# Edge stage of a graph attention layer: visits of eight chunks instead of four, rings of four groups of eight

## The chip, the cores and the metric

One core of a Trainium2 chip runs the kernel. The metric is device time in microseconds for one execution. Engines are named PE (TensorE), DVE (VectorE), ACT (ScalarE), POOL (GpSimd) and SP (SyncE).

## The reference

6250 nodes with 256 features, 206250 edges sorted by destination node (100000 random edges, the same edges reversed, and one loop for each node). All data is float32.

```python
z = einsum('ni,hid->nhd', layernorm(x), W)          # 4 heads of 64
es, ed = (z * a_src).sum(-1), (z * a_dst).sum(-1)
e = leaky_relu(es[src] + ed[dst], 0.01)
alpha = softmax of e over the edges with one dst
x = x + segment_sum(alpha[:, :, None] * z[src], dst)
# then: layernorm, gate to 16 experts, top 2, w1 (256x512), relu, w2, + b2,
# weighted sum, residual, layernorm; x = x + that
```

## The kernel before

The program is a row of stages. Stage A normalises the nodes and multiplies them with W; each node leaves a row of 260 floats in `z_table` in HBM: 256 of z and 4 of es. The edge stage, which the change touches, takes about three quarters of the span. Then come the gate (stage C) and the experts.

In the edge stage a chunk is 128 edges, one to a partition. A group is G = 4 chunks. There are 403 groups (1612 chunks). The nodes are in 49 tiles of 128. A visit is a pair of a group and a node tile for which the group has edges: as the edges are sorted, that is one visit for each group and one more for each end of a tile, VISITS = FULL + NT = 402 + 49 = 451. The tables `visit_tile`, `visit_group`, `visit_word` and `visit_base`, made in stage A, say which group and tile visit v has. `group_free` says how many visits must be over before the buffers of a group may be used again.

The work of the engines in the edge stage:

- POOL, `gather`: for each group it waits on `b_msg` for the messages of an earlier group (four groups back, LEAD = 4), and then issues G indirect DMAs, one for each chunk, each of 128 rows of `z_table` into `ring[:, s, c, :]`. The ring has RING = 8 slots of G chunks.
- SP: for each group `relay` waits until its gathers have landed and counts `b_group` up. For each second group it also loads the destinations of two groups, one row sent to all partitions (`load_pair`, into `dst_bc`), as soon as `make_ST` is done with the groups that lie there, and `relay_pair` waits for that load and counts `b_rows` up. These steps stand in one written order: relay of an even group comes after the relay_pair in front of it.
- DVE, for visit v: `make_ST` (0/1 matrix of node by edge, 128 x G*128), `e_add`, `e_lrelu`, `e_shift`, `e_clamp` (the logits, 128 x 4G), `one_hot` (0/1 matrix of edge by node), `message` (z times weight, 128 x G*256), `accumulate` (adds the sum in PSUM to `acc`).
- PE, for visit v: `destination`, G matmuls that bring ed[dst] to the edges, and `weigh`, G matmuls of 260 columns that add the messages by node into one PSUM tile.
- ACT: `open_group` (copies es out of the ring; it waits for `b_group`), `locate`, `exponent`; near the end also `weight`, which divides finished tiles by their denominators, while DVE's `settle` adds them to x.

The whole stage is written out visit by visit by `written_out`. Each engine goes through iterations i, and in iteration i it runs each of its steps for visit i minus the lag of that step, in the order of the list. On DVE the lag of `make_ST` is 0, of the four logit steps AHEAD = 6, of `one_hot` and `message` AHEAD + 1, and of `accumulate` AHEAD + 1 + MSG_TO_ACC = AHEAD + 3. So `message` of visit v stands on DVE behind `e_add` of visit v + 1. SR = 8 is the number of buffers for S, ST and msg. `destination` of an even visit waits until the logits of visits up to v - SR + 1 are done, since two visits share a PSUM tile (`dest_of`). All of it runs once for each pass; the inputs need one pass.

Of the kernel before, what the change touches and what calls it, by code (L numbers as in the profile page):

```python
# [28 lines left out]
I32 = mybir.dt.int32  # L29
BF16 = mybir.dt.bfloat16  # L30
ALU = mybir.AluOpType
# [1 line left out]
AX = mybir.AxisListType  # L33

P = 128
G = 4
RING = 8
LEAD = 4
SLOPE = 0.01
EPS = 1e-5  # L40
LEVEL = 64.0
# [4 lines left out]
MSG_TO_ACC = 2  # L46
# [1 line left out]
TINY = 1e-30  # L48
RMAX = bass.bass_isa.ReduceOp.max
PAD_DST = 1 << 20  # L50
AHEAD = 6
ZR = 12
SOON = AHEAD + 1

# [49 lines left out]
def gnn_moe_kernel(nc, E, x, x_turned, src_cols, dst_cols, dst_flat, dst_last, W, a_src, a_dst, gate_w, gate_b, w1, b1, w2, b2, gamma, beta, out):  # L104
# [44 lines left out]
    with whole:  # L149
# [23 lines left out]
        visit_tile = sb(graph, "visit_tile", [1, VISITS], I32)  # L173
        visit_group = sb(graph, "visit_group", [1, VISITS], I32)
        visit_word = sb(graph, "visit_word", [1, VISITS], I32)
        group_free = sb(graph, "group_free", [1, GROUPS + RING - LEAD], I32)
        level = sb(graph, "level", [P, HEADS])
        npass_i = sb(graph, "npass_i", [P, 1], I32)

# [43 lines left out]
        with ExitStack() as ctx:  # L223
# [149 lines left out]
            def _(dve):  # L373
# [71 lines left out]
                def aside(t, s, r):  # L445
# [18 lines left out]
                    if t == TABLES + 6:  # L464
                        dve.wait_ge(a_cnt, 2)
                        step(nc.vector.tensor_scalar(visit_base[:, :], psA[1][:, 0:VISITS], -float(P), None, ALU.mult))
                        step(nc.vector.tensor_copy(visit_tile[:, :], psA[1][0:1, 0:VISITS]))
                        step(nc.vector.scalar_tensor_tensor(out=visit_group[:, :], in0=psA[1][0:1, 0:VISITS], scalar=-1.0,
                                                            in1=iota_f[0:1, 0:VISITS], op0=ALU.mult, op1=ALU.add))
                        step(nc.vector.tensor_scalar(visit_slot[:, :], visit_group[:, :], RING - 1, None, ALU.bitwise_and))  # L470
                        step(nc.vector.tensor_copy(visit_word[:, :], visit_slot[:, :]))
                        step(nc.vector.scalar_tensor_tensor(out=visit_word[:, MSG_TO_ACC:VISITS], in0=visit_tile[:, 0:VISITS - MSG_TO_ACC],
                                                            scalar=float(RING), in1=visit_slot[:, MSG_TO_ACC:VISITS], op0=ALU.mult, op1=ALU.add))
                        step(nc.vector.scalar_tensor_tensor(out=visit_word[:, 0:VISITS - SOON], in0=visit_group[:, SOON:VISITS],
                                                            scalar=float(RING * TILE_SPAN), in1=visit_word[:, 0:VISITS - SOON], op0=ALU.mult, op1=ALU.add))
                        step(nc.vector.memset(group_free[:, 0:RING], 0))
                        step(nc.vector.tensor_tensor(group_free[:, RING - 1:GROUPS + RING - LEAD], psA[2][0:1, 0:GROUPS - LEAD + 1],
                                                     iota_f[0:1, 0:GROUPS - LEAD + 1], ALU.add))
                    if t == EARLY + 5:
                        dve.wait_ge(a_edges[0], 16)  # L480
                        step(nc.vector.tensor_scalar(dst_mod[:, :], dst_raw[:, :], P - 1, None, ALU.bitwise_and))
# [60 lines left out]
        b_stats = sem("b_stats"); b_var = sem("b_var")  # L542
        SETTLED = 3 * PART
        CLOSED = VISITS - 1 - (NT - SETTLED)
        assert CLOSED >= 0 and CLOSED + 11 >= 2 * 8 + (VISITS - 2 * 8) // 8 * 8
        SH = 2 * HEADS
        PASS_STEPS = 8
        FIN_STEPS = 2 + BULK - 1
        SR = 8
        with ExitStack() as ctx:  # L550
            nodes = sb(ctx, "nodes", [P, NT, SH])
            decided = sb(ctx, "decided", [P, NT, HEADS])
# [3 lines left out]
            stats_b = decided[:, :, :].rearrange("p t h -> p (t h)")[:, 0:PART * 6].rearrange("p (t c) -> p t c", c=6)  # L556
            ring = sb(ctx, "ring", [P, RING, G, ROW])
            es_edge = sb(ctx, "es_edge", [P, 4, G, HEADS])
            S = xs[:, KEPT:KEPT + 2 * SR, :].rearrange("p (s o) c -> p s (o c)", o=2).rearrange("p s (g e) -> p s g e", g=G)
            ST = xs[:, KEPT + 2 * SR:KEPT + 4 * SR, :].rearrange("p (s o) c -> p s (o c)", o=2)  # L560
            dst_bc = sb(ctx, "dst_bc", [P, RING, G * P], BF16)
            earg = sb(ctx, "earg", [P, 4, 3, G * HEADS])
            msg = sb(ctx, "msg", [P, SR, G, ROW])
# [62 lines left out]
            def _(pool):  # L626
                npass = pool.value_load(npass_i[0:1, 0:1], min_val=1, max_val=PASSES_MAX)
                with pool.Fori(0, npass) as k:
                    def gather(g, s, r):

                        done = pool.value_load(group_free[0:1, bass.ds(g + RING - LEAD, 1)], min_val=0, max_val=VISITS)
                        pool.wait_ge(b_msg, done + 1)
                        pool.sem_inc(apart, 1)
                        for c in range(G):
                            at = src_idx[:, g * G + c:g * G + c + 1]
                            nc.gpsimd.indirect_dma_start(ring[:, s, c, :], None, z_table,  # L636
                                                         bass.IndirectOffsetOnAxis(ap=at, axis=0)).then_inc(b_landed[s], 16)
                    for g in range(GROUPS):
                        gather(g, g % RING, g // RING)
                    pool.sem_inc(b_over, 1)  # L640
                    pool.wait_ge(b_go, k + 1)

            @block.vector
            def _(dve):
# [5 lines left out]
                with dve.Fori(0, npass) as k:  # L650
# [115 lines left out]
                    def accumulate(v, s, r):  # L766
# [5 lines left out]
                        if not early(v, 1):  # L772
                            dve.wait_ge(b_acc, v)
                        at = acc[:, bass.ds(tile, 1), :].rearrange("p o c -> p (o c)")
                        nc.vector.tensor_tensor(at, at, psM[s % 2][:, 0:ROW], ALU.add).then_inc(b_acc, 1)  # L775
                    written_out(VISITS, SR, [(settle, 11), (look_up, AHEAD + 1), (e_add, AHEAD), (make_ST, 0), (e_lrelu, AHEAD),
                                                       (accumulate, AHEAD + 1 + MSG_TO_ACC), (e_shift, AHEAD), (one_hot, AHEAD + 1),
                                                       (e_clamp, AHEAD), (message, AHEAD + 1)])
                    dve.wait_ge(b_acc, VISITS)
# [6 lines left out]
            def _(act):  # L786
                npass = act.value_load(npass_i[0:1, 0:1], min_val=1, max_val=PASSES_MAX)
                with act.Fori(0, npass) as k:
# [29 lines left out]
                    def weight(v, s, r):  # L818
# [5 lines left out]
                        for t in range(n * BATCH, (n + 1) * BATCH):  # L824
# [1 line left out]
                                at = acc[:, t, h * DH:(h + 1) * DH]  # L826
                                last = nc.scalar.activation(at, at, ACT.Copy, scale=rden_b[:, t, h:h + 1])
                            last.then_inc(b_scaled, 1)
                    written_out(VISITS, SR, [(open_group, AHEAD + 2), (locate, AHEAD + 3), (exponent, AHEAD + 3), (weight, 12)])
                    act.sem_inc(b_over, 1)  # L830
                    act.wait_ge(b_go, k + 1)

# [702 lines left out]
```

## Time and profile before

| what | us |
|---|---|
| median of three runs | 2792.49 (2790.86 to 2793.21) |
| the profiled execution, its own time | 2791.16 |
| its span in the profile | 2789.3 |
| busy in the span: PE / DVE / POOL / ACT | 2258.7 / 1711.3 / 1849.1 / 682.4 |
| granted TensorE clock, mean (1 is 2.4 GHz) | 0.821 |
| first gather of the edge stage / last gather | 80.65 / 2126.79 |
| first instruction of stage C | 2147.7 |

Times in the rows are in microseconds from the start of the span, unless they are durations; a mean or a minimum in a row is in ns. A group of instructions has its busy time, the mean of one, and behind the last bar the idle time of the engine just before them with what ended it ("issue" is nothing that the profile shows). A busy engine is not for that reason the bound: the bound is found by following who waits for whom.

### The profile page before, as it was taken

The numbers are of one execution on the slowest core, as the hardware profiler recorded it, in microseconds if no ns is written. First come the engines' busy times: TensorE is split into PE (matmuls) and PEld (weight loads), VectorE is DVE, ScalarE is ACT, GpSimd is POOL, SyncE is SP. The second block draws the span as 40 slices with busy tenths as digits, with TensorE's granted clock in tenths as the row PEclk, the third lists the DMA queues.
The fourth block names the chain that finished last, engine by engine and source line by source line (L and its number), as shares of the span: only waits on it lengthen the run. The fifth ranks groups of instructions, "written<-read, shape, count | busy, mean of one in ns | idle before, by whom it ended". The sixth has DMA issues, their size and how long they took to land. (4 is left out here: it accounts for less than half of the span.)

```text
span 2789.3 us, 54969 instructions
## 1 busy us (share of the span) xinstructions
PE 2258.7 (81%) x10829; PEld 1890.7 (68%) x10830; DVE 1711.3 (61%) x4828; ACT 682.4 (24%) x2857; POOL 1849.1 (66%) x1949
## 2 busy tenths in 40 slices
PE   7688787877878788887888888777884848999997
PEld 5576666666666666666766666666663818999985
DVE  6666666666666666666666666666666674333336
ACT  4111111111111111111111111111115415555557
POOL 0677777777777777777777777777774025555547
PEclk9677888788787887888787788888877559999998
DMA  9444444445454444555454554444554207633328
GB/s 315 121 133 133 130 133 131 133 133 132 132 133 133 133 132 130 133 133 133 133 134 134 133 133 133 132 128 133 134 132 127 87 0 243 197 103 106 107 93 278
DMA packets 183503, 382.70 MB, mean 137 GB/s; under 512 B 38837, under 2 KB 86880, under 8 KB 182474
## 3 DMA queue, kind: packets, MB, share of 16 engines
q0 software_dynamic: 87744, 243.02, 32.6%
q1 hardware_dynamic: 79656, 122.51, 13.7%
q10 hardware_dynamic: 15842, 14.43, 2.0%
q8 instruction: 74, 1.21, 0.2%
q14 instruction: 187, 1.53, 0.2%
HBM read 345.87 MB, written 33.93 MB: 136 GB/s over the span
## 5 line engine op out<-in xcount | busy, mean ns | idle before, releaser
L636 POOL DMA_INDIRECT ring<-z_table,src_idx x1612 | 1556.4, 965 | 496.0 <-issue 458.1
L858 PE MATMUL psMb<-msg,xs 128*128 128x260 f32 x3608 | 1202.5, 491 | 255.4 <-DVE msg L761 253.5
L858 PEld LDWEIGHTS psMb<-msg,xs 128*128 128x128 f32 x3608 | 827.1, 241 | 432.4 <-DVE msg L761 284.0
L847 PEld LDWEIGHTS psEb<-nodes,xs 128*128 128x128 f32 x3608 | 550.0, 224 | 269.3 <-issue 238.2
L847 PE MATMUL psEb<-nodes,xs 128*128 x3608 | 522.7, 272 | 156.5 <-DVE xs L688 155.9
L761 DVE TENSOR_TENSOR msg<-ring,psPb 128x1024 f32<-128x1024 f32 x451 | 546.4, 1211 | 0.0
L807 ACT COPY es_edge<-ring 128x16 f32 x451 | 91.8, 204 | 1679.2 <-SPq L583 1642.6
L702 DVE TENSOR_TENSOR earg<-es_edge,psEb 128x16 f32<-128x16 f32 x451 | 76.1, 169 | 559.5 <-ACT es_edge L807 555.4
L694 DVE TENSOR_TENSOR xs<-iota_f,psPb 128x512 f32<-128x512 f32 x451 | 305.9, 678 | 0.1
L688 DVE TENSOR_SCALAR xs<-dst_bc,iota_p 128x512 f32 x451 | 229.9, 510 | 99.5 <-issue 95.2
L1275 POOL DMA_INDIRECT rows_sb<-norm_rows,src_sb x108 | 109.8, 1017 | 168.1 <-DVE src_sb L1352 149.7
L1307 PE MATMUL psHd<-xT,w_sb 128*128 128x128 f32 x1728 | 213.2, 277 | 0.0
L775 DVE TENSOR_TENSOR acc<-acc,psMb 128x260 f32 x451 | 188.1, 417 | 36.8 <-PE psMb L858 31.4
L1319 PE MATMUL psYd<-w_all,hid 128*128 x864 | 204.4, 380 | 0.3 <-ACT hid L1342 0.3
L1307 PEld LDWEIGHTS psHd<-xT,w_sb 128*128 128x128 f32 x1728 | 204.2, 194 | 0.1
L1363 DVE COPY xT<-psXd 128x256 f32<-128x256 f32 x108 | 45.9, 425 | 255.9 <-PE psXd L1297 255.9
L1319 PEld LDWEIGHTS psYd<-w_all,hid 128*128 128x128 f32 x864 | 156.1, 191 | 17.3 <-issue 0.5
L1330 ACT COPY w_sb<-w_all 128x1024 f32 x108 | 112.8, 1045 | 156.7 <-PE psHd L1307 96.6
L1282 POOL DMA_INDIRECT pair_rows<-y_sb,dst_sb x108 | 107.0, 991 | 45.5 <-issue 36.1
L1342 ACT ACTIVATE hid<-psHd,b1T 128x128 f32<-128x128 f32 x432 | 123.6, 368 | 34.1 <-issue 25.9
L796 ACT ACTIVATE psPb<-dst_col,visit_base 128x4 f32 x451 | 120.5, 267 | 1.4 <-issue 1.4
L814 ACT ACTIVATE msg<-earg 128x16 f32<-128x16 f32 x451 | 91.0, 202 | 54.2 <-DVE earg L720 49.5
(209 smaller groups left out, 1413.3 us busy)
## 6 DMA issues: line engine op xcount, KB each, us to landing
dst_bc<-dst_rows SPq DMA_DIRECT2D x202, 256.0 KB, 3.5
ring<-z_table,src_idx POOLq DMA_INDIRECT x1612
w_all<-in_L_ffn_w_dram SPq DMA_DIRECT2D x32, 512.0 KB
b_sb<-in_L_ffn_b_dram ACTq DMA_DIRECT2D x108, 128.0 KB, 3.1
got<-pair_rows SPq DMA_DIRECT2D x48, 256.0 KB, 4.2
xs<-in_x_dram SPq DMA_DIRECT2D x5, 1536.0 KB, 10.9
z_table<-z_out SPq DMA_DIRECT2D x49, 130.0 KB, 6.3
norm_rows<-xnc SPq DMA_DIRECT2D x49, 128.0 KB, 1.7
```

Of the source, the lines that this page charges most:

```text
L636: nc.gpsimd.indirect_dma_start(ring[:, s, c, :], None, z_table, bass.IndirectOffsetOnAxis(ap=at, axis=0)).then_inc(b_landed[s], 16)
L688: nc.vector.tensor_scalar(ST[:, s, :], dst_bc[:, bass.ds(slot, 1), :].rearrange("p o f -> p (o f)"), iota_p[:, 0:1], None, ALU.is_equal).t ...
L694: nc.vector.tensor_tensor(S[:, s, :, :], over(iota_f[:, 0:P].unsqueeze(1), [P, G, P]), over(psP[s % 2][:, G * HEADS:G * HEADS + G].unsquee ...
L761: nc.vector.tensor_tensor(msg[:, s, :, 0:D].rearrange("p g (h d) -> p g h d", h=HEADS), ring[:, bass.ds(slot, 1), :, 0:D].rearrange("p o g ...
L775: nc.vector.tensor_tensor(at, at, psM[s % 2][:, 0:ROW], ALU.add).then_inc(b_acc, 1)
L796: nc.scalar.activation(psP[s % 2][:, G * HEADS:G * HEADS + G], dst_col[:, bass.ds(group * G, G)], ACT.Identity, bias=visit_base[:, v:v + 1])
L847: last = nc.tensor.matmul(dest_of(s)[:, c * SH:(c + 1) * SH], ST[:, s, c * P:(c + 1) * P], nodes[:, bass.ds(tile, 1), :].rearrange("p o c ...
L858: last = nc.tensor.matmul(psM[s % 2][:, 0:ROW], S[:, s, c, :], msg[:, s, c, :], start=c == 0, stop=c == G - 1)
L1307: last = nc.tensor.matmul(psH[s % 2][:, f * P:(f + 1) * P], w1_sb[:, s % 2, c, f * P:(f + 1) * P], xT[:, s % 2, c, :], start=c == 0, stop= ...
L1319: last = nc.tensor.matmul(psY[s % 2][:, 0:D], hid[:, s % 2, f, :], w2_f, start=f == 0, stop=f == FC - 1)
L1330: nc.scalar.copy(w1_sb[:, s % 2, :, :].rearrange("p c f -> p (c f)"), w_all[:, bass.ds(e, 1), 0:KD * F].rearrange("p o f -> p (o f)")).the ...
L1342: last = nc.scalar.activation(hid[:, s % 2, f, :], psH[s % 2][:, f * P:(f + 1) * P], ACT.Relu, bias=b1T[:, bass.ds(e, 1), f:f + 1].rearran ...
```

## The change

G goes from 4 to 8 and RING from 8 groups to 4, so that the ring holds the same 32 chunks. SR goes from 8 to 4 and AHEAD from 6 to 3, in visits of twice the size. LEAD goes away: a gather waits for the messages of the group four back, which now is the one in the same slot. There are 202 groups (1616 chunks) and VISITS = 201 + 49 = 250. `accumulate` stays two visits behind `message` (MSG_TO_ACC = 2), which are now two visits of eight chunks. PAIRED = RING // 2 goes from 4 to 2 pairs of `dst_bc`, each load twice as large (512 KB over all partitions in place of 256 KB). The lags of `settle` and `weight` are written in terms of AHEAD.

```diff
--- before.py
+++ after.py
@@ -33,9 +33,8 @@
 AX = mybir.AxisListType
 
 P = 128
-G = 4
-RING = 8
-LEAD = 4
+G = 8
+RING = 4
 SLOPE = 0.01
 EPS = 1e-5
 LEVEL = 64.0
@@ -48,7 +47,7 @@
 TINY = 1e-30
 RMAX = bass.bass_isa.ReduceOp.max
 PAD_DST = 1 << 20
-AHEAD = 6
+AHEAD = 3
 ZR = 12
 SOON = AHEAD + 1
 
@@ -173,7 +172,7 @@
         visit_tile = sb(graph, "visit_tile", [1, VISITS], I32)
         visit_group = sb(graph, "visit_group", [1, VISITS], I32)
         visit_word = sb(graph, "visit_word", [1, VISITS], I32)
-        group_free = sb(graph, "group_free", [1, GROUPS + RING - LEAD], I32)
+        group_free = sb(graph, "group_free", [1, GROUPS + 1], I32)
         level = sb(graph, "level", [P, HEADS])
         npass_i = sb(graph, "npass_i", [P, 1], I32)
 
@@ -474,8 +473,8 @@
                         step(nc.vector.scalar_tensor_tensor(out=visit_word[:, 0:VISITS - SOON], in0=visit_group[:, SOON:VISITS],
                                                             scalar=float(RING * TILE_SPAN), in1=visit_word[:, 0:VISITS - SOON], op0=ALU.mult, op1=ALU.add))
                         step(nc.vector.memset(group_free[:, 0:RING], 0))
-                        step(nc.vector.tensor_tensor(group_free[:, RING - 1:GROUPS + RING - LEAD], psA[2][0:1, 0:GROUPS - LEAD + 1],
-                                                     iota_f[0:1, 0:GROUPS - LEAD + 1], ALU.add))
+                        step(nc.vector.tensor_tensor(group_free[:, RING - 1:GROUPS + 1], psA[2][0:1, 0:GROUPS - RING + 2],
+                                                     iota_f[0:1, 0:GROUPS - RING + 2], ALU.add))
                     if t == EARLY + 5:
                         dve.wait_ge(a_edges[0], 16)
                         step(nc.vector.tensor_scalar(dst_mod[:, :], dst_raw[:, :], P - 1, None, ALU.bitwise_and))
@@ -542,11 +541,12 @@
         b_stats = sem("b_stats"); b_var = sem("b_var")
         SETTLED = 3 * PART
         CLOSED = VISITS - 1 - (NT - SETTLED)
-        assert CLOSED >= 0 and CLOSED + 11 >= 2 * 8 + (VISITS - 2 * 8) // 8 * 8
+        assert CLOSED >= 0
         SH = 2 * HEADS
         PASS_STEPS = 8
         FIN_STEPS = 2 + BULK - 1
-        SR = 8
+        SR = 4
+        SPAN = G * P // D
         with ExitStack() as ctx:
             nodes = sb(ctx, "nodes", [P, NT, SH])
             decided = sb(ctx, "decided", [P, NT, HEADS])
@@ -556,8 +556,8 @@
             stats_b = decided[:, :, :].rearrange("p t h -> p (t h)")[:, 0:PART * 6].rearrange("p (t c) -> p t c", c=6)
             ring = sb(ctx, "ring", [P, RING, G, ROW])
             es_edge = sb(ctx, "es_edge", [P, 4, G, HEADS])
-            S = xs[:, KEPT:KEPT + 2 * SR, :].rearrange("p (s o) c -> p s (o c)", o=2).rearrange("p s (g e) -> p s g e", g=G)
-            ST = xs[:, KEPT + 2 * SR:KEPT + 4 * SR, :].rearrange("p (s o) c -> p s (o c)", o=2)
+            S = xs[:, KEPT:KEPT + SPAN * SR, :].rearrange("p (s o) c -> p s (o c)", o=SPAN).rearrange("p s (g e) -> p s g e", g=G)
+            ST = xs[:, KEPT + SPAN * SR:KEPT + 2 * SPAN * SR, :].rearrange("p (s o) c -> p s (o c)", o=SPAN)
             dst_bc = sb(ctx, "dst_bc", [P, RING, G * P], BF16)
             earg = sb(ctx, "earg", [P, 4, 3, G * HEADS])
             msg = sb(ctx, "msg", [P, SR, G, ROW])
@@ -628,7 +628,7 @@
                 with pool.Fori(0, npass) as k:
                     def gather(g, s, r):
 
-                        done = pool.value_load(group_free[0:1, bass.ds(g + RING - LEAD, 1)], min_val=0, max_val=VISITS)
+                        done = pool.value_load(group_free[0:1, bass.ds(g, 1)], min_val=0, max_val=VISITS)
                         pool.wait_ge(b_msg, done + 1)
                         pool.sem_inc(apart, 1)
                         for c in range(G):
@@ -773,7 +773,7 @@
                             dve.wait_ge(b_acc, v)
                         at = acc[:, bass.ds(tile, 1), :].rearrange("p o c -> p (o c)")
                         nc.vector.tensor_tensor(at, at, psM[s % 2][:, 0:ROW], ALU.add).then_inc(b_acc, 1)
-                    written_out(VISITS, SR, [(settle, 11), (look_up, AHEAD + 1), (e_add, AHEAD), (make_ST, 0), (e_lrelu, AHEAD),
+                    written_out(VISITS, SR, [(settle, AHEAD + 2 + MSG_TO_ACC), (look_up, AHEAD + 1), (e_add, AHEAD), (make_ST, 0), (e_lrelu, AHEAD),
                                                        (accumulate, AHEAD + 1 + MSG_TO_ACC), (e_shift, AHEAD), (one_hot, AHEAD + 1),
                                                        (e_clamp, AHEAD), (message, AHEAD + 1)])
                     dve.wait_ge(b_acc, VISITS)
@@ -826,7 +826,7 @@
                                 at = acc[:, t, h * DH:(h + 1) * DH]
                                 last = nc.scalar.activation(at, at, ACT.Copy, scale=rden_b[:, t, h:h + 1])
                             last.then_inc(b_scaled, 1)
-                    written_out(VISITS, SR, [(open_group, AHEAD + 2), (locate, AHEAD + 3), (exponent, AHEAD + 3), (weight, 12)])
+                    written_out(VISITS, SR, [(open_group, AHEAD + 2), (locate, AHEAD + 3), (exponent, AHEAD + 3), (weight, AHEAD + 4)])
                     act.sem_inc(b_over, 1)
                     act.wait_ge(b_go, k + 1)
 
```

## Rows read from the trace of the kernel before

**Rows 1.** Busy time and count by stretch, granted clock, DMA share, GB/s.

```profile
80.00:97.00 17.00, 0.00 (x0) 0.00 (x0) 15.59 (x14) 1.49 (x2) 14.83 (x6) 0.50 0.30 94
97.00:2128.00 2031.00, 1645.89 (x7193) 1358.52 (x7193) 1341.11 (x3615) 298.60 (x1892) 1541.52 (x1607) 0.81 0.50 132
```

**Rows 2.** The gathers, line 636, from 97 to 2128 us: group, durations, idle before.

```profile
L636 POOL DMA_INDIRECT ring<-z_table,src_idx x1607 | 1541.8, 959 | 489.5 <-issue 456.9 <-DVE msg L761 32.6
...
L636 POOL DMA_INDIRECT ring<-z_table,src_idx x1607: 942/946/1583, 96.7 to 2126.8; - x179
...
  DVE msg L761: 32.6, 107
```

**Rows 3.** Who waited for whom, 97 to 2128 us: total, times, longest.

```profile
SPq L583 <- DMA ring<-z_table,src_idx: 1178.6, 401, 7.9
SPq L597 <- DMA dst_bc<-dst_rows: 635.2, 198, 3.9
...
DVE earg L702 <- ACT es_edge L807: 552.8, 333, 3.4
```

**Rows 4.** DVE's groups of instructions, 97 to 2128 us.

```profile
L761 DVE TENSOR_TENSOR msg<-ring,psPb 128x1024 f32<-128x1024 f32 x449 | 543.9, 1211 | 0.0
L694 DVE TENSOR_TENSOR xs<-iota_f,psPb 128x512 f32<-128x512 f32 x449 | 304.6, 678 | 0.1
L688 DVE TENSOR_SCALAR xs<-dst_bc,iota_p 128x512 f32 x451 | 229.9, 510 | 99.5 <-issue 95.2 <-PE psEb L847 3.7
L775 DVE TENSOR_TENSOR acc<-acc,psMb 128x260 f32 x447 | 186.4, 417 | 34.0 <-PE psMb L858 29.5 <-issue 3.5
L720 DVE TENSOR_SCALAR earg<-earg 128x16 f32<-128x16 f32 x450 | 86.2, 192 | 0.0
L702 DVE TENSOR_TENSOR earg<-es_edge,psEb 128x16 f32<-128x16 f32 x450 | 76.0, 169 | 556.9 <-ACT es_edge L807 552.8 <-PE psEb L847 2.9 <-issue 0.8
```

**Rows 5.** PE's groups, 97 to 2128 us.

```profile
L858 PE MATMUL psMb<-msg,xs 128*128 128x260 f32 x3585 | 1194.9, 491 | 252.2 <-DVE msg L761 250.3
L847 PE MATMUL psEb<-nodes,xs 128*128 x3608 | 522.7, 272 | 156.5 <-DVE xs L688 155.9
```

**Rows 6.** Timeline (start, duration): two pairs of make_ST and gather.

```profile
203.56 0.49 DVE L688 TENSOR_SCALAR xs<-dst_bc,iota_p 128x512 f32 x1 [0.27 <-issue]
203.66 1.21 POOL L636 DMA_INDIRECT ring<-z_table,src_idx  x1 [0.31 <-issue]
...
1003.51 0.49 DVE L688 TENSOR_SCALAR xs<-dst_bc,iota_p 128x512 f32 x1 [0.27 <-issue]
1003.52 0.94 POOL L636 DMA_INDIRECT ring<-z_table,src_idx  x1 [0.30 <-issue]
```

**Rows 7.** Loads by SP: one in time, landing of dst_bc, of other loads.

```profile
304.70 0.20 ACT L807 COPY es_edge<-ring 128x16 f32 x1 [2.12 <-SPq L583]
305.13 0.32 SPq L586 DMA_DIRECT2D dst_bc<-dst_rows  x1
...
DMA to landing us min/median/max: 3.1/3.5/4.3
...
acc<-in_x_turned_dram SPq DMA_DIRECT2D x12, 512.0 KB, 9.2
xs<-in_x_dram SPq DMA_DIRECT2D x3, 512.0 KB, 6.6
```

**Rows 8.** Timeline of the stage's end.

```profile
2126.79 0.95 POOL L636 DMA_INDIRECT ring<-z_table,src_idx  x1 [0.30 <-issue]
2130.46 0.17 DVE L702 TENSOR_TENSOR earg<-es_edge,psEb 128x16 f32<-128x16 f32 x1 [2.60 <-ACT es_edge L807]
2134.03 8.70 ACT L827 ACTIVATE acc<-acc,pass_tmp 128x64 f32<-128x64 f32 x36
2137.46 2.02 PE L858 MATMUL psMb<-msg,xs 128*128 128x260 f32 x8 [0.58 <-DVE msg L761]
2139.62 0.42 DVE L775 TENSOR_TENSOR acc<-acc,psMb 128x260 f32 x1 [1.89 <-PE psMb L858]
```

## The prediction

> **What bounds the kernel now.** I read the busy times by stretch first. The edge stage's body runs from 97 to 2128 us, 2031 us of a span of 2789, and in it no engine is busy throughout: PE 1646, POOL 1542, DVE 1341 [rows 1]. Busy shares alone would point at PE. So next come the waits. DVE waits 553 us at `e_add` for ACT's copy of es [rows 3], ACT waits for SP's relay, and SP waits 1179 us for gathers to land [rows 3]. The chain leads to POOL. Its own group shows 1607 gathers of 959 ns in the mean, with 489.5 us of idle time, that is 0.305 us before each [rows 2]. Is this idle time a wait? 107 of the gaps are put down to `message`, but they too are 32.6/107 = 0.30 us long [rows 2], no longer than the others, which end on nothing that the profile shows. So POOL issues gathers back to back, one each 1.264 us (2031/1607), at group boundaries as elsewhere. 0.946 (the median) + 0.305 = 1.251 would be the period without disturbance; the mean of 959 is 13 ns over the median, in all 21 us over 1607 gathers. The edge stage lasts as long as POOL takes to issue its gathers, plus the way of the last one through the other engines. What the change does to DVE, PE, ACT and SP is worth nothing unless it reaches one of these: the number of gathers, their period, the end.
>
> **What disturbs a gather.** At 203.56 `make_ST` (line 688) begins, 0.10 us before a gather, and ends 0.39 us after the gather's start; that gather takes 1.21 us. At 1003.51 `make_ST` begins 0.01 us before a gather, and that one takes 0.94 [rows 6]. So a `make_ST` that is already under way holds the start of the gather up: 1.21 - 0.946 = 0.26 us for an end 0.39 us behind the start, hence delay = (end behind the start) - 0.13. With D the length of `make_ST` and starts spread evenly over a period of 1.25 us, one of them costs (D - 0.13)^2 / 2.5. For D = 0.49 [rows 6] (the mean of 0.510 in [rows 4] has `make_ST`'s own delays in it) that is 0.052 us, times 451 = 23 us, against the 21 found above. The two agree, so I take this as the source of the excess.
>
> The Trainium skill, page "SBUF — State Buffer", section "SBUF: two separate sides", has such a rule: a DVE instruction in a 2-port mode, or with two SBUF inputs, takes the port pair shared with GpSimd for the whole instruction, and GpSimd cannot write descriptors meanwhile. The slow gather agrees with it; the 0.94 us gather beside a `make_ST` started just before does not fit a lock over both whole instructions. Held strictly, the rule would charge each `make_ST` its full length: 250 of them by the 0.80 us worked out below, near 200 us.
>
> **The change, part by part.** The sum is made against the profiled execution, 2791.16 us (span 2789.3); the median of the runs is 1.3 us above it.
>
> 1. Gathers. 202 groups of 8 are 1616, 403 groups of 4 were 1612. The four more are padding but are issued. POOL: 4 x 1.25 = +5.0 us, all on the path.
>
> 2. Group overhead on POOL (value_load, wait, counter) is halved, but it costs nothing now: the gap is 0.30 us inside groups and between them. 0 us. It could give at most nothing, as there is no longer gap to remove.
>
> 3. `make_ST`. A 16-wide instruction of this kind costs 0.192 (line 720), the 512-wide one 0.49 [rows 4, 6], so 0.30/496 = 0.60 ns an element, and 1024 cost 0.80 us. Half as many, each longer. Evenly spread: 0.67^2/2.5 = 0.18 us x 250 = 45 us, against 21 to 23: +22 to +24. But the starts are not spread evenly: `make_ST` follows `e_add`, and that follows the landing of a group's last gather, so most are at nearly one phase of POOL's period. [rows 6] show how narrow it is: 0.10 us before the gather costs 0.26 us, 0.01 before costs nothing. In the new kernel a hit at that phase costs 0.80 - 0.10 - 0.13 = 0.57 us, a miss nothing. For some 75 visits (second visits of a group and those behind an SP load) I take the even 0.18: 13 us. For the other 175, the even cost of 0.052 in the old kernel over a hit's 0.26 makes one in five a hit: 35 x 0.57 = 20 us. Together 33 us, against 21: +12 us. Bounds: no hit at all, -21 us; a hit each time for the 175, 100 + 13 - 21 = +92 us. I take +12, nearest to what the rows show on average.
>
> By the Trainium skill, page "VectorE: DVE Perf Modes", section "Mode 2×_2P — use both read ports for one tensor", such a one-input float32 result comes two elements a cycle at 0.96 GHz, so 512 more would be an estimated 0.27 us, not 0.31. The trace's slope is close to this. By the page the sum would be some 4 us less.
>
> 4. DVE. `message` over 2048: 1.211 + 1024 x (1.211 - 0.417)/764 = 2.28 us; `one_hot` 0.678 + 0.53 = 1.21; `make_ST` 0.80; `accumulate` 0.417 as before; four small ones some 0.19 each [rows 4]. That is 5.4 us a visit, 250 visits 1350 us, against 3.5 x 451 = 1579. DVE is relieved of some 229 us, off the path: it had 553 us of waiting for gathers, and it gets more. For a group of 8 (8 x 1.264 = 10.1 us of POOL) it has 1.24 visits, 6.7 us. 0 us.
>
> 5. PE. 2000 chunk visits by 0.491 + 0.272 [rows 5] are 1526 us, before 1804, 1376. +150 us, covered by the idle time of the body (2031 - 1646 = 385 us). Without that cover up to +150. `destination` of an even visit now waits for `e_clamp` of the third visit before it, in the same DVE iteration; before, that was an iteration back. It is late by about 2.5 us, and what is queued behind it on PE is `weigh`, whose message isn't ready sooner. 0 us.
>
> 6. SP. With AHEAD = 3, `make_ST` at the landing T of odd group g builds the visit three further on. If no group near is split, that is group g+3, in the pair that SP loads only after T. The issue is 0.43 us behind the es copy (304.70 to 305.13); 256 KB land in 3.5 us, other loads of 512 KB in 6.6 and 9.2 [rows 7]. Bounds 3.5 and 9.2, I take 5, since this one is the old load doubled; with the relay `make_ST` starts near T + 6.5. Behind it on DVE are `one_hot` and `message`, so the iteration ends at T + 11; the next group lands at T + 10.1 and its iteration is over at T + 16.5, before T + 20.2, the landing after it. Three whole groups without a tile's end are 1 - 3/4.1, about a quarter of the pairs. Does POOL feel it? A gather of group g+4 needs the last message of g, which stands behind `e_add` of g+1. The last gather before a landing starts 3.7 us ahead of it (2126.79 to 2130.46 [rows 8]), so gather g+4 starts 20.2 - 3.7 + 1.25 = 17.8 us after T(g+1). Message g ends 5.4 us after T(g+1), or 11 to 12 behind a late load. POOL doesn't wait: 0 us. Cover gone if the load takes over some 11 us.
>
> 7. The end. From the last `e_add` (2130.46) to ACT's last `weight` (2134.03 + 8.70) it was 12.3 us; DVE ended at 2139.62 + 0.42 [rows 8]. New: two iterations of DVE behind the landing, the last message some 8.5 us after it, then 8 matmuls of 0.505 (2.02/4) and `accumulate`: 13.1 us. ACT has fewer `weight` blocks left and is no longer last. +1 us (up to +6 if PE is at its lower clock there). The stage's head (six gathers up to 97 us [rows 1]) stays.
>
> Sum: 5.0 + 12 + 1 = +18 us. Against the profiled execution that is 2809; the median could lie 1 us higher, which I leave in the range.
>
> **The rivals.** What this kernel can tell from no change is 0.2%, 5.6 us.
> - *Fewer `make_ST`, fewer hits: faster.* 250 in place of 451, and their phase falls just behind a gather's start. For it: the phase is narrow and a longer es copy and `e_add` move it later, towards the harmless side. Against: DVE time under `make_ST` stays near 200 us. At no hits: 2791 + 6 - 21 = 2776. It decides if the disturbance falls below 9 us of the old 21. Chance 0.12.
> - *No change.* Hits as before: 2797, or a few less. Chance 0.18, for a sum within 5.6 us of the old.
> - *Phase locked on the bad side.* 2791 + 92 + 6: 2889; half of it 2843. For it: nearly all landings now have one phase. Chance 0.10 for over 2835.
> - *Late destination rows.* Landing of 512 KB over 11 us: POOL waits in a quarter of the 101 pairs, 2 us each for 13 us, +50: 2859. Against: 9.2 is the slowest row of that size. Chance 0.04.
> - *PE becomes the bound.* The body's granted clock is 0.81, between the levels of 1.2 and 2.4 GHz [rows 1]. 1.24 visits of 8 chunks cost 7.6 us of the 10.1 at that mean. At the lower level throughout, 0.81/0.5 of it, 12.3 us: +2.2 x 202 = 440 us. Against: PE would then have no idle time, and in the body it has 385 us. Chance 0.03.
>
> **How the numbers follow.** The likeliest case, slower by a longer hold on POOL and four more gathers, has 0.53; it gives 2809. With the three worse ones slower has 0.70, no change 0.18, faster 0.12. The likeliest case's own range is 2798 to 2830. For 8 in 10 I leave out the bad lock, the late rows and PE above (0.13 or so beyond 2838), and half of the faster case below: 2788 to 2838.
>
> **What would show it.** 1616 gathers, gap before each still 0.30; median duration 0.946 still, with fewer but longer slow ones (up to 1.5 us) and a mean near 966; `make_ST` near 0.80 us; DVE's busy time down by 200 us and its wait for es up; the body at 1616 periods. I am wrong if POOL shows gaps over 0.31 put down to `message`, if SP's wait for `dst_bc` has single values over 10 us, or if the mean gather comes below 950 ns.

## The result: 28 us slower, where 18 were forecast

The changed kernel takes 2819.88 us in the median (2818.54 to 2821.84, four runs), the kernel before beside it 2791.99. The ratio is 1.010 with an interval of 1.0087 to 1.0113. So the change makes the kernel 1.0% slower, by more than its runs scatter. The forecast was 2809, with 2788 to 2838 around it, and 0.70 for slower.

The page of the changed kernel, its span and engines:

```profile
span 2817.4 us, 46496 instructions
## 1 busy us (share of the span) xinstructions
PE 2313.0 (82%) x11613; PEld 1988.1 (71%) x11614; DVE 1589.9 (56%) x3220; ACT 566.7 (20%) x2053; POOL 1871.5 (66%) x1953
```

The busy times by stretch, to be read against [rows 1]:

```profile
78.00:95.00 17.00, 0.00 (x0) 0.00 (x0) 15.59 (x14) 0.00 (x0) 14.80 (x6) 0.50 0.30 94
95.00:2150.00 2055.00, 1699.38 (x7960) 1453.10 (x7961) 1219.79 (x2013) 190.78 (x1114) 1564.43 (x1611) 0.81 0.46 131
```

The body has grown by about 24 us, with PE busier (1699 us), DVE less so (1220), and POOL as before the engine without a wait of its own. Its gathers from 97 us on, beside the first row of [rows 2]:

```profile
L636 POOL DMA_INDIRECT ring<-z_table,src_idx x1610 | 1563.6, 971 | 490.4 <-issue 445.9 <-DVE msg L761 44.5
```

Mean 971 ns instead of 959; 490.4 us of gaps over 1610 gathers are 0.305 us each, as before, and none of the 1616 gathers has more than 0.31 us before it. So the gaps have not changed; the gathers themselves have become longer. The waits of the other engines in the same stretch, in the form of [rows 3], first by engine, then by SP's queue:

```profile
DVE earg L702 <- ACT es_edge L807: 652.9, 198, 6.6
...
DVE xs L688 <- SPq L597: 121.3, 28, 5.1
...
POOL ring L636 <- DVE msg L761: 44.5, 146, 0.3
```

```profile
SPq L583 <- DMA ring<-z_table,src_idx: 1577.9, 201, 18.4
SPq L597 <- DMA dst_bc<-dst_rows: 370.6, 99, 4.6
```

DVE waits 100 us longer for landings than it did. 28 times `make_ST` waits for SP's load of destination rows, 4.3 us each. The load itself, with the new `make_ST` (durations in ns, minimum, median, maximum; the last row is in us):

```profile
L688 DVE TENSOR_SCALAR xs<-dst_bc,iota_p x250: 737/754/960, 95.0 to 2124.5; 128x1024 f32 x125
...
DMA to landing us min/median/max: 3.5/4.0/4.9
```

PE and DVE by group, beside [rows 4, 5]:

```profile
L858 PE MATMUL psMb<-msg,xs 128*128 128x260 f32 x3960 | 1203.2, 470 | 121.1 <-DVE msg L761 119.9
...
L761 DVE TENSOR_TENSOR msg<-ring,psPb 128x2048 f32<-128x2048 f32 x248 | 564.3, 2276 | 0.0
...
L847 PE MATMUL psEb<-nodes,xs 128*128 x3996 | 538.4, 271 | 233.7 <-DVE earg L720 196.2 <-DVE xs L688 37.2
L694 DVE TENSOR_TENSOR xs<-iota_f,psPb 128x1024 f32<-128x1024 f32 x248 | 299.9, 1209 | 0.0
L688 DVE TENSOR_SCALAR xs<-dst_bc,iota_p 128x1024 f32 x248 | 189.8, 765 | 167.4 <-SPq L597 121.3 <-issue 45.2 <-PE psEb L847 0.8
L775 DVE TENSOR_TENSOR acc<-acc,psMb 128x260 f32 x246 | 102.0, 415 | 6.7 <-PE psMb L858 6.4
```

**Where the 28 us are.** The boundaries are the first gather, the last gather and the first instruction of stage C, in the two profiled executions (before, after):

| stretch | before | after | more |
|---|---|---|---|
| start to first gather | 80.65 | 78.68 | -2.0 |
| first to last gather | 2046.1 | 2070.2 | +24.0 |
| last gather to stage C (2147.7 and 2177.2) | 20.9 | 28.4 | +7.5 |
| stage C to the end | 641.6 | 640.2 | -1.4 |
| span | 2789.3 | 2817.4 | +28.1 |

The 24.0 us split again. Four more gathers at 1.25 us are 5.0. In the timeline of before, 116 of the 1607 gathers from 97 us on take 0.99 us or more, together 22.0 us over 0.946; in that of after it is 128 of 1610 and 40.8 us: +18.8. Together 23.8.

Which `make_ST` are behind the long gathers? Three pairs from the timeline of after, one of each kind (start, duration). The excess of a gather is its duration less the median of 0.946:

```profile
606.11 0.74 DVE L688 TENSOR_SCALAR xs<-dst_bc,iota_p 128x1024 f32 x1
606.41 1.25 POOL L636 DMA_INDIRECT ring<-z_table,src_idx  x1 [0.30 <-DVE msg L761]
...
868.50 1.11 POOL L636 DMA_INDIRECT ring<-z_table,src_idx  x1 [0.30 <-issue]
868.73 0.75 DVE L688 TENSOR_SCALAR xs<-dst_bc,iota_p 128x1024 f32 x1 [4.33 <-SPq L597]
...
874.76 0.75 DVE L688 TENSOR_SCALAR xs<-dst_bc,iota_p 128x1024 f32 x1 [0.25 <-issue]
874.90 1.43 POOL L636 DMA_INDIRECT ring<-z_table,src_idx  x1 [0.30 <-issue]
```

At 606.11 `make_ST` belongs to the second visit of a split group, where DVE does not wait; it ends 0.44 us after the gather has started, and the gather takes 1.25. At 868.73 it had waited 4.33 us for SP, begins 0.23 us after a gather and costs it 0.16. At 874.76 it follows a landing, ends 0.61 us behind the gather's start, and the gather takes 1.43. Counted over the whole timeline:

| `make_ST` of after | number | gathers lengthened | us together |
|---|---|---|---|
| behind a wait for the landing | 168 | 47 | 18.6 |
| behind a late load by SP | 28 | 23 | 3.9 |
| with no wait (second visits) | 51 | 51 | 16.6 |

Three `make_ST` lie outside the stretch. In the kernel before it was 68 of 332 behind a landing with 14.3 us, and 46 of 117 others with 6.9. Most of the rest, in both kernels, are two or three gathers beside `settle`'s multiplications of 1.0 us (0.8 us of excess before, 1.5 after).

The three pairs also show that there are two places in a gather where a `make_ST` holds it up. The first is the one of the prediction: a `make_ST` under way 0.1 us before the gather's start costs (end behind the start) - 0.13, which is 0.31 for the pair at 606 and 0.48 for that at 874. The pair at 868 is of another kind, as this `make_ST` began after the gather. It ends 0.98 us behind the gather's start, and the gather is 0.16 longer: (end behind the start) - 0.83. In the timeline of after 37 `make_ST` begin 0 to 0.5 us behind a gather's start and end more than 0.83 behind it. All 37 gathers are lengthened, each by that difference within 0.03 us, together by 6.6 us. In the kernel before, where a `make_ST` is 0.49 us long and seldom reaches so far, it was 19 gathers with 1.9 us. So of the 18.8 us some 13.5 are more excess at the first place, 4.7 at the second, and 0.7 beside `settle`.

The first gathers have grown too. The sixth and the seventh gather of the stage took 0.95 and 0.94 us before; now they start at 94.70 and 96.16 and take 1.15 and 1.64. That is 0.9 us, which the slightly shorter ordinary gathers make up for in the sum above.

The end of the stage, beside [rows 8]:

```profile
2148.86 0.95 POOL L636 DMA_INDIRECT ring<-z_table,src_idx  x1 [0.30 <-issue]
2153.94 0.19 DVE L702 TENSOR_TENSOR earg<-es_edge,psEb 128x32 f32<-128x32 f32 x1 [6.13 <-ACT es_edge L807]
...
2157.55 2.96 ACT L827 ACTIVATE acc<-acc,pass_tmp 128x64 f32<-128x64 f32 x12
...
2158.49 9.18 PE L858 MATMUL psMb<-msg,xs 128*128 128x260 f32 x32 [5.35 <-DVE msg L761]
...
2159.82 2.28 DVE L761 TENSOR_TENSOR msg<-ring,psPb 128x2048 f32<-128x2048 f32 x1
...
2167.81 0.42 DVE L775 TENSOR_TENSOR acc<-acc,psMb 128x260 f32 x1 [3.08 <-PE psMb L858]
...
2177.28 0.21 DVE L1057 TENSOR_SCALAR rden<-acc 128x52 f32<-128x52 f32 x1 [9.04 <-PEq L550]
```

From the last gather to `e_add` it is 5.08 us, before 3.67. From there to the last engine's end 14.29 (DVE, 2168.23), before 12.27 (ACT). The last message ends 8.16 us behind `e_add`. But then PE is still in the `weigh` of the visit before, which began at 2158.49 and takes until 2164.2 at a granted clock of 0.66; the last `weigh` takes 3.4 us more, at 1.00, the higher of the two levels. From the last engine's end to stage C it is 9.0, before 5.0. What lies in this last piece shows in POOL's drain at the end of the block (line 550; ns, then the start), in the kernel after and in the kernel before:

```profile
L550 POOLq DRAIN  x1: 6601/6601/6601, 2170.4 to 2170.4; - x1
```

```profile
L550 POOLq DRAIN  x1: 2354/2354/2354, 2145.1 to 2145.1; - x1
```

All engines come to this point at 2170.4 and at 2145.1; all but POOL are through at once, and POOL's drain takes 6.6 us where it took 2.35. It ends last, 0.2 us ahead of stage C, in both.

The 2 us at the start are as much as the tables of stage A save: twelve DVE instructions over 200 to 250 columns where there were 400 to 451, in all 4.4 us instead of 6.5. That these are the cause is argued, not shown; the first gather of the unaltered changed kernel starts at 78.7 here and at 77.7 in `g1`.

### The profile page after: what moved, and what is told of

Its sections match the earlier page's. It is cut to its first block and busy times, and to the rows that moved or that the text cites. A ratio compares the mean times of both kernels' runs of the same rounds, so it can differ in the third digit from the quotient of the medians.

```text
span 2817.4 us, 46496 instructions
## 1 busy us (share of the span) xinstructions
PE 2313.0 (82%) x11613; PEld 1988.1 (71%) x11614; DVE 1589.9 (56%) x3220; ACT 566.7 (20%) x2053; POOL 1871.5 (66%) x1953
## 3 DMA queue, kind: packets, MB, share of 16 engines
q8 instruction: 76, 1.25, 0.2%
## 5 line engine op out<-in xcount | busy, mean ns | idle before, releaser
L636 POOL DMA_INDIRECT ring<-z_table,src_idx x1616 | 1579.2, 977 | 497.4 <-issue 447.4
L858 PEld LDWEIGHTS psMb<-msg,xs 128*128 128x128 f32 x4000 | 934.0, 240 | 322.0 <-DVE msg L761 133.5
L761 DVE TENSOR_TENSOR msg<-ring,psPb 128x2048 f32<-128x2048 f32 x250 | 568.9, 2276 | 0.0
L702 DVE TENSOR_TENSOR earg<-es_edge,psEb 128x32 f32<-128x32 f32 x250 | 46.2, 185 | 664.4 <-ACT es_edge L807 659.0
L807 ACT COPY es_edge<-ring 128x32 f32 x250 | 54.4, 218 | 1773.3 <-SPq L583 1751.5
L694 DVE TENSOR_TENSOR xs<-iota_f,psPb 128x1024 f32<-128x1024 f32 x250 | 302.3, 1209 | 0.0
L688 DVE TENSOR_SCALAR xs<-dst_bc,iota_p 128x1024 f32 x250 | 191.3, 765 | 168.7 <-SPq L597 121.3
L775 DVE TENSOR_TENSOR acc<-acc,psMb 128x260 f32 x250 | 103.7, 415 | 12.1 <-PE psMb L858 11.7
L957 POOL TENSOR_TENSOR high<-high,tile_h 128x1972 bf16<-128x1972 bf16 (+1 forms) x6 | 20.1, 3349 | 110.4 <-DVE high L1204 110.4
L814 ACT ACTIVATE msg<-earg 128x32 f32<-128x32 f32 x250 | 54.0, 216 | 81.3 <-DVE earg L720 79.1
```

Source lines behind the costliest of these rows:

```text
L688: nc.vector.tensor_scalar(ST[:, s, :], dst_bc[:, bass.ds(slot, 1), :].rearrange("p o f -> p (o f)"), iota_p[:, 0:1], None, ALU.is_equal).t ...
L694: nc.vector.tensor_tensor(S[:, s, :, :], over(iota_f[:, 0:P].unsqueeze(1), [P, G, P]), over(psP[s % 2][:, G * HEADS:G * HEADS + G].unsquee ...
L761: nc.vector.tensor_tensor(msg[:, s, :, 0:D].rearrange("p g (h d) -> p g h d", h=HEADS), ring[:, bass.ds(slot, 1), :, 0:D].rearrange("p o g ...
L858: last = nc.tensor.matmul(psM[s % 2][:, 0:ROW], S[:, s, c, :], msg[:, s, c, :], start=c == 0, stop=c == G - 1)
```

## The experiments

Five chips took part. On the one of the first pair and on the one of the last run, the kernel before took 2792 and 2789 us. On the three others it took 3465, 3508 and 3528. There, engines stood still in the edge stage with no releaser in the profile: in the unaltered changed kernel on the third of them (`g1`), PE's two groups have 1089 us of idle time that ends on nothing that the profile shows. These are some of its rows, single matmuls of 0.17 us with 2.6 us before each:

```profile
1047.69 0.17 PE L847 MATMUL psEb<-nodes,xs 128*128 x1 [2.61 <-issue]
1050.50 0.17 PE L847 MATMUL psEb<-nodes,xs 128*128 x1 [2.64 <-issue]
1053.32 0.17 PE L847 MATMUL psEb<-nodes,xs 128*128 x1 [2.65 <-issue]
```

On those three chips POOL waits some 700 us for `message`, and what lengthens a gather is partly hidden. Durations of single instructions can be compared; total times there say little about a chip on which POOL sets the pace. The kernel before, unaltered, has no trace on these three. The code below is shortened: `dst_bc[slot]` stands for the whole access to that slot, `half q` for one half of the columns, `head h` for the 64 columns of a head.

**e1 and f1: `make_ST` in two halves**, in the changed kernel.

```diff
-nc.vector.tensor_scalar(ST[:, s, :], dst_bc[slot], iota_p, None, ALU.is_equal).then_inc(b_ST, 1)
+for q in range(2):   # 512 of the 1024 columns each
+    made = nc.vector.tensor_scalar(ST[:, s, half q], dst_bc[slot, half q], iota_p, None, ALU.is_equal)
+made.then_inc(b_ST, 1)
```

> The changed kernel with each make_ST written as two instructions of 512 columns (0.49 us each) instead of one of 1024 (0.75 us). Theory of the hold: POOL's gather waits for the instruction under way, so a hit costs at most 0.36 us in place of 0.6; the excess over 0.946 us per gather falls from 41 us to about 19, and the time from 2820 to about 2797. Rival, the extra time comes from the two-visit lag and the late destination rows (28 waits for SP, 121 us on DVE): DVE only gets 60 us more work, so the time stays at 2820 or rises.

> The changed kernel with each make_ST in two instructions of 512 columns, once more, since on the first chip engines stood still in this stage for reasons outside the kernel. Theory of the hold: 41 us of excess in the gathers fall to about 19, the time from 2820 to about 2797. Rival (two-visit lag, late destination rows): no gain, 2820 or more.

Measured: 3490.0 and 3528.0 us, 1.0073 (1.005 to 1.0097) and 1.0051 (1.0021 to 1.0082) of the time before, on two of the chips with stalls. The changed kernel had not run there, so on the time this tells neither theory from the other. The gathers of e1, from its page:

```profile
L636 POOL DMA_INDIRECT ring<-z_table,src_idx x1616 | 1553.4, 961 | 1169.4 <-DVE msg L764 688.0
```

59 gathers are over 0.99 us, 11.1 us together, in f1 52 with 9.3.

**g1 and g2: the changed kernel and its halved form on one chip.**

> The changed kernel, unaltered, so that the next two stand beside it on one chip. On a chip like the first pair's: 1.010 of the time before. On one where engines stand still between instructions, as in the last eight runs: POOL then waits for messages and the hold matters less, 1.00 to 1.01.

> The changed kernel with make_ST in two halves. Where POOL's gathers set the pace, the theory of the hold says 24 us less than the changed kernel (0.8%); the rival says no gain. Where they don't, both say no difference.

Measured: 3539.0 and 3541.0 us, 1.0011 (0.9981 to 1.0041) and 1.0037 (1.0011 to 1.0064) of the time before. The gathers of g1 and g2, from their pages:

```profile
L636 POOL DMA_INDIRECT ring<-z_table,src_idx x1616 | 1566.2, 969 | 1234.9 <-DVE msg L761 743.8
```

```profile
L636 POOL DMA_INDIRECT ring<-z_table,src_idx x1616 | 1552.2, 961 | 1234.3 <-DVE msg L764 740.0
```

In g1 108 gathers are over 0.99 us with 23.5 us of excess, in g2 54 with 9.7. So halving `make_ST` takes more than half of the excess away. The time doesn't follow here (2 us more instead of 14 less); POOL waits 744 and 740 us for messages in between. The rivals can't be told apart by the time on this chip; by the gathers the hold is confirmed.

**e2: `make_ST` of double length.** The comparison is written as a tensor_tensor with two inputs in SBUF; it takes 1.21 us.

```diff
-nc.vector.tensor_scalar(ST[:, s, :], dst_bc[slot], iota_p[:, 0:1], None, ALU.is_equal)
+nc.vector.tensor_tensor(ST[:, s, :], dst_bc[slot], over(iota_p[:, 0:1], [P, G * P]), ALU.is_equal)
```

> The changed kernel with make_ST as a tensor_tensor of dst_bc and iota_p, two inputs in SBUF, one element a cycle: about 1.2 us instead of 0.75. Theory of the hold: if two SBUF inputs hold POOL as the four instructions on acc do at 82 us, the excess of the gathers rises from 41 to about 140 us, the time to about 2915. Rival (no hold, late rows): DVE has 650 us of waiting left and hides 110 us, 2820.

Measured: 3526.2 us, one run, beside 3464.9 of before and 3490.0 of e1 on that chip. Its gathers:

```profile
L636 POOL DMA_INDIRECT ring<-z_table,src_idx x1616 | 1615.5, 1000 | 1158.0 <-DVE msg L761 660.6
```

183 gathers over 0.99 us, 72.9 us of excess, the longest 2.00 us. The unaltered length has 21.6 to 24.4 us on these chips (`e3`, `f3`, `g1`), so the rise is some 50 us, half of what I expected, which is in keeping with a kernel in which POOL is idle more often. This edit changes two things at once, the length and the second input in SBUF, so it does not show the length alone at work. In order of the length of one `make_ST`, on chips with stalls: 0.49 us gives 9 to 11 us of excess, 0.75 gives 21.6 to 24.4, 1.21 gives 73. The rival, late rows, changes none of these. The order doesn't go on below that: with 0.35 us, two to each visit of four chunks, it is 14 to 16 us (`e4` and its like, below), as more gathers are hit, 123 to 138 instead of 52 to 59, at 0.11 us each.

**e3 and f3: no gathers for padding**, in the changed kernel.

```diff
-for c in range(G):
+for c in range(min(G, CHUNKS - g * G)):
```

SP's `relay` counts four landings fewer for the last group.

> The changed kernel without the four gathers that hold only padding: 1612 gathers. Theory: 5.0 us of POOL less, and the last landing 1.4 us sooner if gathering one row 128 times is what delays it: 2813.5. If also POOL's drain at the end of the stage (28 us after the last gather's start, against 21 before the change) hangs on these four gathers, another 4 to 6 us: 2808. Rival: the padded gathers are hidden, 2820.

> The changed kernel without its four padding gathers, once more. Theory: 5.0 us of gathers, 1.4 us of landing and 0.3 us of POOL's drain less: 2813. Rival: hidden, 2820.

Measured: 1.004 (1.0012 to 1.0069) and 1.002 (0.9993 to 1.0048) of the time before. The changed kernel had not run on these two chips, so the time shows no saving or loss by the edit. The end shows in the timeline. Last gather and es copy of f3, then the es copy of the changed kernel, whose last gather starts at 2148.86:

```profile
2829.22 0.95 POOL L637 DMA_INDIRECT ring<-z_table,src_idx  x1 [0.30 <-issue]
...
2832.67 0.22 ACT L808 COPY es_edge<-ring 128x32 f32 x1 [1.54 <-SPq L584]
```

```profile
2153.69 0.22 ACT L807 COPY es_edge<-ring 128x32 f32 x1 [8.25 <-SPq L583]
```

3.45 us instead of 4.83, as in the kernel before (2126.79 to 2130.22, 3.43). So it is the four gathers of padding, 128 times the same row each, that made the last landing 1.4 us later. With them it was 5.41 us in `g1` and 5.42 in `h1`, so here the delay is 2.0. POOL's drain in e3, 0.33 us shorter than 6.60:

```profile
L550 POOLq DRAIN  x1: 6274/6274/6274, 2830.0 to 2830.0; - x1
```

**e4 and f2: `make_ST` in halves in the kernel before. f4 and g3: also the head's multiplications cut in seven.**

```diff
-nc.vector.tensor_tensor(acc[:, :, head h], acc[:, :, head h], over(decided[:, :, h:h + 1], [P, NT, DH]), ALU.mult)
+for q in range(0, NT, 7):
+    nc.vector.tensor_tensor(acc[:, q:q + 7, head h], acc[:, q:q + 7, head h], over(decided[:, q:q + 7, h:h + 1], [P, 7, DH]), ALU.mult)
```

> The kernel before the change with each make_ST written as two instructions of 256 columns. Theory of the hold: the excess falls from 22 us to about 7, the time from 2792 to about 2778. Rival: DVE gets 80 us more work in a stage in which it waits 553 us, no change, 2792.

> The kernel before with each make_ST in two instructions of 256 columns, once more. Theory of the hold: excess from 22 to about 7 us, 2792 to about 2778. Rival: no change.

> The kernel before with make_ST in two instructions of 256 columns, and with each of the four multiplications of acc by decided at the stage's head (3.3 us each, two inputs in SBUF) in seven of 7 tiles. Theory: the first gathers, which take 3.0 to 4.0 us each under them, fall to at most 1.5 us; 6 to 8 us less than the kernel with make_ST alone split, about 2771. Rival: the whole DVE stretch holds POOL whatever its cuts, as DVE takes the port up again at once: no gain over 2778.

> The kernel before with make_ST in halves and the head's multiplications in sevenths. Where POOL's gathers set the pace: 15 us from the first and 7 us from the second, 0.992 of the time before. Rival: 1.000.

Measured against the kernel before: e4 1.0006 (0.9987 to 1.0025); f2 0.9924 (0.990 to 0.9949) and f4 0.9937 (0.9904 to 0.997) on one chip; g3 0.9899 (0.9851 to 0.9948). Excess of the gathers: 14.2, 15.0, 16.0 and 15.9 us; I had expected 7. Whether that is less than the kernel before has on these chips isn't known: the changed kernel's excess is 40.8 us on the first chip and 23.5 in `g1`, and the 22 us of the kernel before may be as much smaller there. The head's gathers, uncut (f2) and cut (f4):

```profile
81.46 3.99 POOL L636 DMA_INDIRECT ring<-z_table,src_idx  x1 [0.30 <-issue]
85.76 3.02 POOL L636 DMA_INDIRECT ring<-z_table,src_idx  x1 [0.30 <-issue]
```

```profile
82.86 1.19 POOL L636 DMA_INDIRECT ring<-z_table,src_idx  x1 [0.30 <-issue]
84.36 1.29 POOL L636 DMA_INDIRECT ring<-z_table,src_idx  x1 [0.30 <-issue]
```

The first eight gathers start over 18.5 us in f2 and over 11.3 us in f4 and g3, so cutting an instruction with two SBUF inputs gives POOL its turn between the pieces: the rival of f4 falls. The 7 us don't show between f2 and f4. The kernel before with halves was faster than unaltered by 0.6 to 1.0% in `f2`, `f4` and `g3` and the same in `e4`, all on chips with stalls. By the medians that is 20, 26 and 32 us. The excess of the gathers can have fallen by some 7 us only (22 less 15), and the head by another 7 in `f4` and `g3`, so most of the gain isn't explained by the hold. That this version beats the kernel before on a chip without stalls wasn't measured.

**h1: a second wait and counter on POOL in each group of eight.**

```diff
 for c in range(G):
+    if c == G // 2:
+        pool.wait_ge(b_msg, done + 1)
+        pool.sem_inc(apart, 1)
```

> The changed kernel with a second wait and counter step on POOL between the fourth and the fifth gather of a group, as often as in the kernel before. POOL's drain at the stage's end is 6.60 us in every kernel with groups of eight (6.27 without the padding gathers) and 2.35 in every one with groups of four. If it depends on how many gathers follow each other without such a step, it falls to about 2.4 us here; if on the four semaphores of the ring in place of eight, or on the number of groups, it stays at 6.60. If the chip is one where POOL sets the pace: 2820 less at most 4; otherwise the time is that of the changed kernel.

Measured: 2817.53 us beside 2789.05, ratio 1.0104 (1.0087 to 1.0121), on a chip without stalls. Its gathers (118 over 0.99 us, 38.0 us of excess) and its drain:

```profile
L639 POOL DMA_INDIRECT ring<-z_table,src_idx x1616 | 1578.0, 976 | 497.4 <-issue 446.7
```

```profile
L550 POOLq DRAIN  x1: 6597/6597/6597, 2169.7 to 2169.7; - x1
```

The drain stays. The number of gathers between two waits isn't what sets it. And the loss of 1% is there again on a second chip without stalls, with the same signs, in a kernel that differs by the extra wait.

## Why the prediction was right in direction and short by 11 us

- *POOL sets the pace, through the number of gathers and their period* (the first part): right. No gap over 0.31 us in 1616 gathers, with 11% more matmuls on PE (4000 rows a group for 3608), DVE 121 us less busy (1711.3 to 1589.9; I had 229) and SP's load late 28 times. None of it reached POOL.
- *DVE, 229 us less*: the sum added means of instructions that overlap a little. In the body their durations add up to 1584 us before and to 1333 after, 251 less, but DVE's busy time is only 1341 and 1220.
- *PE, +150, covered*: the reading was wrong. Each chunk of a visit leaves two rows in each of PE's groups (3608 for 1804), and the rows overlap, so 0.491 + 0.272 is not the cost of a chunk. The busy time gives 1725 us for 1804, 0.956 each, and 1754 us for 2000, 0.877 each. Why a chunk became cheaper stays open. The wait of `destination` for `e_clamp` came as described, 196 us of PE's idle time, and did not reach POOL. By 0.956 PE would have needed 1.24 x 8 x 0.956 = 9.5 us of the 10.1 that POOL takes for a group, not the 7.6 that the rival "PE becomes the bound" gives it; it needed 1754/202 = 8.7. That PE stayed covered was a closer thing than the prediction says, and partly luck.
- *Four gathers, +5.0*: right; they cost 1.25 us each, and 1.4 us more at the landing, which I had not seen.
- *A longer hold by `make_ST`, +12*: right in kind, mis-sized, +18.8. `make_ST` takes 0.754 us in the median where I had 0.80. For those behind a landing I had 20 us from 35 hits; it was 18.6 from 47 hits. For the 75 others I had 13 us, from starts spread evenly; it was 20.5 from 79 `make_ST`, 74 of them hits. The step that was mis-sized is "for some 75 visits I take the even 0.18". In a second visit `make_ST` follows the chain of DVE's instructions from the landing without a wait, so it has a fixed phase as well: 35 of these 79 start 0.3 us before a gather, and all 51 second visits delay one. The other fault is in the rule for the delay, which knows only a `make_ST` under way at the gather's start: a longer one reaches the second place, 0.83 us behind that start, and this made 6.6 us where it had been 1.9. The estimate of 0.27 us more for 512 columns, from the Trainium skill's page "VectorE: DVE Perf Modes", section "Mode 2×_2P — use both read ports for one tensor", was nearer to the measured 0.754 - 0.487 than my slope. The sum by it would have been 3 us less, not 4: 35 x 0.04 and 75 x (0.67^2 - 0.63^2)/2.5.
- *The strict lock* (each `make_ST` charged in full, near 200 us): not so here. The excess is 40.8 us, and half of the 247 `make_ST` in the stretch lengthen no gather. I also gave that rule too widely. For two SBUF inputs the Trainium skill's page "SBUF — State Buffer", section "SBUF: two separate sides", limits it to a GpSimd operation that reads SBUF. What the runs show of two such inputs is `f2` and `f4`: gathers of 3.0 to 4.0 us under multiplications of 3.4, and of 1.2 to 1.3 under pieces of 0.5.
- *Late destination rows*: the mechanism came as described, 28 `make_ST` of about 4.3 us (I had a quarter of 101 pairs). The load took 4.0 us, where I had taken 5. POOL never waited for it. But 23 of these late `make_ST` lengthened a gather, by 3.9 us together, which is part of the 20.5 above.
- *The end, +1*: mis-sized, +7.5. 1.4 us is the landing. 2.0 is the chain behind the last `e_add`, where I had 0.8 (14.3 us against 13.1): the last message ended 8.2 us behind `e_add`, for which I had 8.5, but the last `weigh` had to wait 2.1 us for that of the visit before. 4.0 is the time from there to stage C, which ends with POOL's drain, a term missing altogether.
- *The head stays*: not quite, two of its gathers were lengthened by 0.9 us. The 2 us less ahead of the first gather were not in the sum.
- The span grew by 28.1 us, 10.1 over the sum of 18: +6.8 in the hold, +6.5 at the end, +0.2 not placed (two longer gathers in the head, +0.9, against slightly shorter ordinary ones), against -2.0 and -1.4 in stages that I took as unchanged. The -1.4 from stage C on isn't explained.

The link between hold and time is shown by the profile: between the first gather and the last there are only gathers and equal gaps, so what lengthens a gather lengthens the stage. The link between the length of `make_ST` and the gathers is shown by the pairs in the timeline and by e1, f1, g1 and g2. That halving `make_ST` gives time back where POOL sets the pace was not measured, since all those runs fell on chips with stalls. Left open: why POOL's drain is 2.35 us in all kernels with 403 groups of four and eight ring semaphores, and 6.6 in those with 202 groups of eight and four semaphores; and what makes engines stand still on three of five chips.

## What to carry to other kernels

Find the engine that issues without a pause, and ask of a change first what it does to that engine's count, period and tail; bigger pieces that save fixed costs elsewhere can lengthen the one thing that it shares with them. Where two engines take turns at something, the length of the single instruction counts, not only its sum, and a chain without waits has a fixed phase: look for it before you average over phases. At the end of a stage count also what padding does to the last transfer, and the drain.

## What the runs showed of the hardware

- A `make_ST` that is under way 0.1 us before a gather issued by POOL makes that gather longer by its end behind the gather's start, less 0.13 us (within 0.03 us for 85 of 89 in the kernel after). One that begins up to 0.5 us behind the gather's start and ends more than 0.83 us behind it makes it longer by its end less 0.83 us (37 of 37). The 121 others cost nothing. `message`, with one input in PSUM, takes 1.21 us in the kernel before, and of the 73 gathers of over 1.1 us there in the body none overlaps one. Multiplications with two SBUF inputs of 3.4 us made gathers of 3.0 to 4.0 us; in pieces of 0.5 us they take 1.2 to 1.3.
- With four gathers whose 128 indices are all one row as the last of the stage, es is copied 4.83, 5.41 and 5.42 us behind the last gather's start (after, g1, h1); without them 3.45 in both f3 and e3.
- POOL's drain at the end of the block took 2.354 us in all five kernels with groups of four (before, e4, f2, f4, g3), 6.60 us in all seven with groups of eight and padding (after, e1, e2, f1, g1, g2, h1), and 6.274 without the padding (e3, f3), with stalls and without.
- One program took 2792 and 2789 us on two chips and 3465 to 3528 us on three. The changed kernel took 2819 and 3553 us in its two profiled executions; of the 734 us between them some 725 lie between the first gather and stage C, in idle time like that shown of g1.
